# First attention of a two-layer block: four buffers of results, single maxima between the scores, parts of the maxima kept in PSUM

## The reference, cut to what matters

```python
A1 = jnp.einsum('bhqd,bhkd->bhqk', Q1, K1) * scaling
A2 = jnp.einsum('bhqd,bhkd->bhqk', Q2, K2) * scaling
A1 = jnp.where(causal, A1, neg_inf)
A2 = jnp.where(causal, A2, neg_inf)
attn = jax.nn.softmax(A1, -1) - lam * jax.nn.softmax(A2, -1)
O = jnp.einsum('bhqk,bhkd->bhqd', attn, V)
```

## Time and profile before

| | before |
|---|---|
| median of three executions | 4490.27 us |
| lowest and highest | 4481.56 and 4502.51 us |
| the profiled execution | 4483.99 us (span 4481.8 us) |
| mean granted clock of TensorE | 0.902 |
| TensorE busy, whole span | 3649.0 us (81%) |
| VectorE, ScalarE, GpSimd busy | 2374.4, 1656.8, 1702.6 us |
| the attention stage | 354 to 2777 us |

### The profile page before, as it was taken

How to read it: one execution, slowest core, us unless ns; L and a number is a source line. 1 busy time by engine, 2 the same in 40 slices (tenths; PEclk the granted TensorE clock), 3 DMA queues, 4 the chain that set the end, 5 groups by cost and what they waited for, 6 DMA issues and landing times. The chain is left out here.

```text
span 4481.8 us, 84217 instructions
## 1 busy us (share of the span) xinstructions
PE 3649.0 (81%) x28333; PEld 1946.0 (43%) x28335; DVE 2374.4 (53%) x4499; ACT 1656.8 (37%) x3266; POOL 1702.6 (38%) x1117
## 2 busy tenths in 40 slices
PE   6868888998988888888898897762799768897694
PEld 3323344443434343434344443662455434555463
DVE  4457566565656565656566560776511176666202
ACT  2314555555555555555555555110022132111110
POOL 1313454554545454545454555420144332110112
PEclk8978999999999999999999998775699989997797
DMA  4430101111111111111111111210233310001333
GB/s 151 154 113 24 41 25 42 26 40 28 38 30 35 32 34 34 31 37 25 42 26 40 27 26 51 103 48 11 90 90 76 59 34 4 0 0 38 108 100 92
DMA packets 229259, 224.74 MB, mean 50 GB/s; under 512 B 88721, under 2 KB 198546, under 8 KB 222738
## 3 DMA queue, kind: packets, MB, share of 16 engines
q1 hardware_dynamic: 213522, 194.33, 14.7%
q0 software_dynamic: 15360, 25.44, 2.9%
HBM read 138.58 MB, written 80.35 MB: 49 GB/s over the span
## 5 line engine op out<-in xcount | busy, mean ns | idle before, releaser
L692 DVE TENSOR_REDUCE attention_chunk_max<-attention_ps_m 128x1 f32<-128x512 f32 (+3 forms) x2560 | 1386.9, 603 | 892.1 <-PE attention_ps_m L795 451.0
L637 POOL TENSOR_TENSOR attention_probs<-attention_probs 128x1024 f32<-128x1024 f32 (+2 forms) x640 | 1225.9, 1916 | 1281.5 <-PE attention_ps_o L770 1281.5
L670 ACT ACTIVATE attention_probs<-attention_ps_s 128x512 f32<-128x512 f32 (+3 forms) x2560 | 1241.6, 536 | 939.3 <-PE attention_ps_s L745 481.9
L741 PE MATMUL attention_ps_s<-attention_q_stack,attention_k_stack 99*128 99x512 bf16 (+3 forms) x2560 | 836.6, 358 | 176.3 <-ACT attention_probs L670 155.5
L792 PE MATMUL attention_ps_m<-attention_k_stack,attention_q_stack 96*128 96x512 bf16 (+3 forms) x2560 | 811.3, 360 | 152.6 <-DVE attention_chunk_max L692 98.4
L770 PE MATMUL attention_ps_o<-attention_probs,attention_v_head 128*32 128x256 f32 (+1 forms) x9728 | 657.4, 376 | 0.5 <-ACT attention_probs L670 0.4
L792 PEld LDWEIGHTS attention_ps_m<-attention_k_stack,attention_q_stack 96*128 96x128 bf16 x2560 | 248.5, 99 | 524.5 <-DVE attention_chunk_max L692 357.7
L741 PEld LDWEIGHTS attention_ps_s<-attention_q_stack,attention_k_stack 99*128 99x128 bf16 x2560 | 223.2, 98 | 524.1 <-ACT attention_probs L670 259.3
L781 PE MATMUL attention_ps_o<-attention_probs,consts 128*32 128x256 f32 (+1 forms) x5120 | 432.6, 369 | 0.4 <-POOL attention_probs L637 0.4
L770 PEld LDWEIGHTS attention_ps_o<-attention_probs,attention_v_head 128*32 128x32 f32 x9728 | 268.1, 112 | 273.7 <-ACT attention_probs L670 100.4
L781 PEld LDWEIGHTS attention_ps_o<-attention_probs,consts 128*32 128x32 f32 x5120 | 204.4, 113 | 90.3 <-issue 13.5
(11 more groups left out here) (276 smaller groups left out, 3979.6 us busy)
## 6 DMA issues: line engine op xcount, KB each, us to landing
qk_parts<-project_parts SPq DMA_DIRECT2D x64, 384.0 KB, 3.0
heads_out<-attention_results_sb SPq DMA_DIRECT2D x256, 64.0 KB
out_heads<-heads_out SPq DMA_DIRECT2D x8, 2048.0 KB, 7.9
experts_w<-in_f_w SPq DMA_DIRECT2D x16, 1024.0 KB, 8.3
attention_q_stack<-qk_parts SPq DMA_DIRECT2D x32, 384.0 KB
attention_k_stack<-qk_parts SPq DMA_DIRECT2D x32, 384.0 KB
experts_w<-in_e_w SPq DMA_DIRECT2D x24, 512.0 KB, 4.9
v_rows<-project_v SPq DMA_DIRECT2D x8, 1024.0 KB
```

What stands on the lines that cost most here:

```text
L637: pool.tensor_tensor(probs[:, to, :, lo:], probs[:, to, :, lo:], probs[:, k % RING_P, :, lo:], ALU.add).then_inc(pair_ok, 1)
L670: act.activation(probs[:, k % RING_P, a, left(k):], ps_s[(2 * k + a) % RING_S][:, left(k):], ACT.Exp, scale=float(DH) ** -0.5).then_inc(pr ...
L692: last = dve.tensor_reduce(chunk_max[:, a, jq, c:c + 1], ps_m[m % RING_M][:, 0:width(m)], AX.X, ALU.max)
L741: last = pe.matmul(psum[:, lo:], ks[at][0:WITH_MAX, a, kb * P:(kb + 1) * P], qs[at][0:WITH_MAX, a, tq * GROUP + lo:(tq + 1) * GROUP], star ...
```

## The change

- Results: four buffers in SBUF (`RING_R`) and four semaphores `stored` instead of two; a `take` waits for the store of the same turn of the head before. PSUM keeps two (`RING_O`).
- `take` moves from ahead of exponential (k, 1), four steps behind a turn's end, to ahead of exponential (k, 0), five steps behind it.
- The maxima of a pair are cut in four shares (of four: one each; of five: 1, 1, 1, 2). Order in an iteration: score (k + 2, 0), score (k + 2, 1), first share, score (k + 3, 0), second share, `values`, `ones`, third share, score (k + 3, 1), fourth share. In the last pair, the next head's scores (0, 0) and (0, 1) come ahead of the first share and (1, 0) behind the third.
- The split of the maxima works in place in PSUM: no `max_rest`, four chained operations, and the PSUM buffer is released behind the fourth (it was behind the second).

```diff
--- before.py
+++ after.py
@@ -501,16 +501,15 @@
 
 
     with stage(nc, "attention0") as s:
-        RING_P, RING_S, RING_M, RING_O = 8, 3, 3, 2
+        RING_P, RING_S, RING_M, RING_O, RING_R = 8, 3, 3, 2, 4
         qs = [s.sb(f"q_stack{i}", [P, 2, N], BF16) for i in range(STACKS)]
         ks = [s.sb(f"k_stack{i}", [P, 2, N], BF16) for i in range(STACKS)]
         vh = [s.sb(f"v_head{i}", [P, K_TILES, DV], F32) for i in range(STACKS)]
         probs = s.sb("probs", [P, RING_P, 2, GROUP], F32)
-        results = s.sb("results_sb", [P, RING_O, 2, BLOCKS, P], F32)
+        results = s.sb("results_sb", [P, RING_R, 2, BLOCKS, P], F32)
         chunk_max = s.sb("chunk_max", [P, 2, K_TILES, Q_TILES], F32)
         neg_max = s.sb("neg_max", [P, 2 * K_TILES], F32)
         max_parts = s.sb("max_parts", [2 * K_TILES, 3, P], BF16)
-        max_rest = s.sb("max_rest", [2 * K_TILES, P], F32)
         ps_s = [s.ps(f"ps_s{i}", [P, GROUP]) for i in range(RING_S)]
         ps_m = [s.ps(f"ps_m{i}", [P, GROUP]) for i in range(RING_M)]
         ps_o = [s.ps(f"ps_o{i}", [P, 2, BLOCKS, P]) for i in range(RING_O)]
@@ -519,7 +518,7 @@
         (ready, score_ok, prob_ok, values_ok, pair_ok, ones_ok, max_ok, max_used, steps, neg_ok, parts_ok,
          parts_in, taken) = (s.sem(n) for n in names)
         loaded = [s.sem(f"loaded{i}") for i in range(STACKS)]
-        stored = [s.sem(f"stored{i}") for i in range(RING_O)]
+        stored = [s.sem(f"stored{i}") for i in range(RING_R)]
         block = s.engines()
         N_STEPS, N_MAX = len(STEPS), len(MAXIMA) + 1
         LOADS = len(RUNS[0]) + len(RUNS[1]) + 1
@@ -606,7 +605,7 @@
 
             def store(head, turn):
 
-                tile, slot = TURNS[turn - 1], (turn - 1) % RING_O
+                tile, slot = TURNS[turn - 1], (turn - 1) % RING_R
                 h = head - 1 if turn == 0 else head
                 h = h if isinstance(h, int) else sp.snap(h)
                 wait_apart(sp, taken, head * Q_TILES + turn + RING_O, core.passed)
@@ -619,12 +618,12 @@
                         results[half * 2 * DV:(half + 1) * 2 * DV:DV, slot, 1]).then_inc(stored[slot], 16)
 
 
-            for slot in range(RING_O):
+            for slot in range(RING_R):
                 sp.sem_inc(stored[slot], STORES * 16)
             sp.sem_inc(parts_in, 48)
             run(sp, step)
-            for slot in range(RING_O):
-                sp.wait_ge(stored[slot], STORES * 16 * (1 + HEADS * Q_TILES // RING_O))
+            for slot in range(RING_R):
+                sp.wait_ge(stored[slot], STORES * 16 * (1 + HEADS * Q_TILES // RING_R))
 
         @block.gpsimd
         def _(pool):
@@ -645,14 +644,11 @@
             act.sem_inc(taken, RING_O)
 
             def take(head, turn):
-                slot = turn % RING_O
-                if isinstance(head, int):
-                    act.wait_ge(stored[slot], ((head * Q_TILES + turn) // RING_O + 1) * (STORES * 16))
-                else:
-                    act.wait_ge(stored[slot], (head * (Q_TILES // RING_O) + turn // RING_O + 1) * (STORES * 16))
+                slot = turn % RING_R
+                act.wait_ge(stored[slot], (head * (Q_TILES // RING_R) + 1) * (STORES * 16))
                 act.wait_ge(values_ok, head * N_STEPS + LAST[turn] + 1)
                 act.wait_ge(ones_ok, head * PAIRS + (LAST[turn] + 1) // PAIR + RING_P // PAIR)
-                act.activation(results[:, slot], ps_o[slot][:], ACT.Copy).then_inc(taken, 1)
+                act.activation(results[:, slot], ps_o[turn % RING_O][:], ACT.Copy).then_inc(taken, 1)
 
             def step(at_head, after, later):
                 if at_head is None:
@@ -660,8 +656,8 @@
                 head = at_head.n
                 for k in range(N_STEPS):
                     for a in range(2):
-                        ended = ends(k, 4)
-                        if a == 1 and ended and not (ended[1] and is_first(head)):
+                        ended = ends(k, 5)
+                        if a == 0 and ended and not (ended[1] and is_first(head)):
                             take(head - 1 if ended[1] else head, ended[0])
                         act.wait_ge(score_ok, head * 2 * N_STEPS + 2 * k + a + 1)
                         if k % PAIR == 0 and a == 0:
@@ -697,17 +693,17 @@
                         dve.tensor_reduce(neg_max[:], chunk_max[:].rearrange("p a j c -> p (a j) c"), AX.X, ALU.max,
                                           negate=True).then_inc(neg_ok, 1)
 
-                        chain = Counted(dve, steps, after * 2)
+                        chain = Counted(dve, steps, after * 4)
                         m = len(MAXIMA)
                         psum = ps_m[m % RING_M][0:2 * K_TILES, 0:P]
                         dve.wait_ge(max_ok, after * N_MAX + m + 1)
                         dve.wait_ge(parts_in, (after + 1) * 48)
                         chain.then(dve.tensor_copy(max_parts[:, 0], psum))
-                        dve.tensor_tensor(max_rest[:], psum, max_parts[:, 0], ALU.subtract).then_inc(max_used, 1)
-                        dve.wait_ge(max_used, after * N_MAX + m + 1 + RING_M)
-                        chain.then(dve.tensor_copy(max_parts[:, 1], max_rest[:]))
-                        dve.tensor_tensor(max_parts[:, 2], max_rest[:], max_parts[:, 1], ALU.subtract)\
-                            .then_inc(parts_ok, 1)
+                        chain.then(dve.tensor_tensor(psum, psum, max_parts[:, 0], ALU.subtract))
+                        chain.then(dve.tensor_copy(max_parts[:, 1], psum))
+                        chain.then(dve.tensor_tensor(max_parts[:, 2], psum, max_parts[:, 1], ALU.subtract))
+                        dve.sem_inc(parts_ok, 1)
+                        dve.sem_inc(max_used, 1)
 
             def step(at_head, next_head, later):
                 if at_head is None:
@@ -824,30 +820,31 @@
                     if whose is not None and (k == BEGIN_MAX or k == 0 and is_first(head)):
                         pe.wait_ge(loaded[whose_at], (whose.round + 1) * (LOADS * 16))
                     more = k + 2 < N_STEPS
-                    third = -(-len(items) // 3)
+                    share = [items[n * len(items) // 4:(n + 1) * len(items) // 4] for n in range(4)]
                     if more:
                         score(head, at, k + 2, 0)
-                        maxima(whose_n, whose_at, items[:third])
                         score(head, at, k + 2, 1)
-                        maxima(whose_n, whose_at, items[third:2 * third])
+                    maxima(whose_n, whose_at, share[0])
+                    if more:
                         score(head, at, k + 3, 0)
                     elif after is not None:
 
                         pe.wait_ge(parts_in, (after + 2) * 48)
-                        maxima(whose_n, whose_at, items[:2 * third])
                         score(after, other, 0, 0)
+                        score(after, other, 0, 1)
+                    maxima(whose_n, whose_at, share[1])
                     values(head, at, k)
                     values(head, at, k + 1)
                     if k > 0:
                         ones(head, k // PAIR - 1)
                     elif not is_first(head):
                         ones(head - 1, PAIRS - 1)
+                    maxima(whose_n, whose_at, share[2])
                     if more:
                         score(head, at, k + 3, 1)
                     elif after is not None:
-                        score(after, other, 0, 1)
                         score(after, other, 1, 0)
-                    maxima(whose_n, whose_at, items[2 * third:])
+                    maxima(whose_n, whose_at, share[3])
                     if after is not None and k == END_MAX:
                         turn_maxima(after)
                 if after is None:
```

## The result

The changed kernel takes 4107.76 us, the median of four executions (4102.68 to 4111.56), against 4491.16 for the kernel before on the same chips (four executions now). The ratio is 0.9145 with a 95% interval of 0.9121 to 0.9169. That is 383 us less, where 405 were forecast, and inside the likeliest case's own range. The profiled execution has a span of 4104.3 us.

The account below looks back on a forecast made before the run. TensorE's own order of work and its waits bound the attention stage. Gains of 206 + 190 + 7 = 403 us gave 4081 from the profiled 4483.99 and 4087 from the median 4490.27; forecast 4085 us, range 4035 to 4195.

Parts of the forecast that it names:

- likeliest case: Whole kernel: all gains arrive, 4085 us, own range 4040 to 4150, chance 0.72.
- The store stall: ScalarE's copy of results: four buffers end its wait for the store, gaining 206 us, bounds 177 and 231.
- The order: TensorE's pairs of steps: single maxima between scores gain 190 us, bounds 0 and 227; heads 0 and 30 add about 7.
- the 0.5 us for exponentials: TensorE's undisturbed head: 0.5 us added for waits on exponentials, within the forecast 62.0 us.
- The turn of the loop: Turn of the three-head loop: 0.8 us of the mean head's loss, read apart from the clock's 1.0.
- The copy one exponential later: ScalarE's four copies a head: moving them costs nothing; without the move the third score waits some 0.5 us at each.
- The parts in PSUM: VectorE's split of the maxima: casts from PSUM at 0.28 us instead of 920 ns, 0 on the path.
- (a): Rival: the stall goes but waits for exponentials replace those for maxima, so the order brings nothing; 4284 us, chance 0.06.
- (c, d): Rivals at step 20: TensorE waits for a later head's loads; c 4175 us, chance 0.06; d slower, 4560 us, chance 0.02.
- (b): Rival: half of the gain from TensorE's new order is lost; 4184 us, chance 0.10.
- (e): Rival: a copy still waits for a store because SyncE is blocked longer; order gives its 190; 4293 us, chance 0.03.
- under 50 us: Profile sign: TensorE's wait for the maxima in the attention stage falls under 50 us.

Follow-up runs that it names:

- the run with the early wait: The changed kernel with one more TensorE wait, for the loads of the head after the next already at step 12 instead of 20: 4372.33 us.
- the run with the scores in a row: The changed kernel with no maxima between the scores, two shares ahead of the values and two behind the sums: 4304.72 us.

## Why the prediction was right, point by point

**The store stall.** Forecast 206 us, measured 202 alone. Putting an undisturbed head together from a disturbed one and the one head without loads gave 68.54 us, and the chip gave 68.53.

**The order.** Forecast 190 + 7 us on top of the buffers, measured 4289.1 - 4107.8 = 181. The undisturbed head came out at 62.36 us where 62.0 was forecast, 0.36 x 29 = 10 us. It wasn't the 0.5 us for exponentials: the matmuls' waits for them are 4.8 us in the stage, 0.17 a head. Part of it is in the price of the columns. The sum has 14.7 us each for scores and maxima, 68 times 512 columns; at its own price of 0.22 that is 15.0, and the head would have been 62.5. No row separates the rest. Also, four pairs of 19 have five maxima, not a quarter of them, and nothing hangs on that. What the gain is made of was seen in part: of 6.2 us a head 1.8 are the wait behind the split of the maxima (the prediction had about 1.5 for it), and the other 4.4 the bursts in the pairs. The heads outside the loop gave a little more than forecast: head 0 went from 87.64 to 80.25 us, and heads 30 and 31 together gave 2.3, where 7 was forecast for head 0 and head 30.

**The turn of the loop: the term that was mis-sized.** I took the turn's 0.8 us a head over unchanged. It is 63.78 - 62.36 = 1.42 after, and 0.6 x 29 = 18 us went there. In rows: TensorE's eight gaps are 26.1 us where they were 16.1, and behind a gap of 3.4 us it runs at 1.2 GHz (0.53) for as long. Before the change the granted clock stayed at 1.00 through four of the eight turns; after it, it fell at all eight. In the profiled executions the gain is 12.71 x 29 + 7.4 (head 0) + 2.3 (heads 30 and 31) = 378 us where 403 were forecast: 10 and 18 us less by these two items, 3 more by the heads outside the loop. The loop is the cause of the gaps (two turns, two gaps; no loop, no gap), and the loads' DMAs are not. The order makes them longer: they are 25.7 us with the order alone and 18.0 with the buffers alone. Why it does stays open; what I have not tried is what TensorE has queued at the branch.

**The copy one exponential later.** Nothing on the path, as forecast. But I wrote that without the move the third score would wait 0.5 us at each copy, and the run without it shows no cost that can be told from none (4111.39 against 4107.16 us). The step that failed: I priced the copy against the old order, where the score follows the sums at once, and not against the new, where a maximum stands between them.

**The parts in PSUM.** 0, as forecast. On VectorE alone the move pays: 278 against 920 ns for the same cast, and the 920 were the end of GpSimd's sum, as the rows of the two engines in the section on the result show. In the new order that is 0.65 us a head that nobody waits for.

**The rivals.** The exponentials (a) had their price right, 0.42 us a pair, and their condition too: it falls due only without maxima between the scores. The loads (c, d) decided nothing, by 4 to 5 us in a typical head and by about 1 us in the tightest, and the run with the early wait shows that they are through 27.2 us behind their issue, where I had read 27.1 from the store blocked behind them. A stall that moves did show, but in the order alone: 47 us are missing there, 28.5 of them in ScalarE's longer wait. Of (b) and (e) nothing came: the order brought 181 of its 197 us, and no copy waits for a store.

**What the profile was to show.** The clock is 0.99 in the stage, not 1.00, because of the loop's turns (without the loop it is 1.00 from 361.5 to 2307.3 us). Pairs of four full maxima take 3.34 us. The forecast of "under 50 us" for TensorE's waits for maxima is right for matmuls (3.6 us) and wrong for weight loads (181.0 us). It should have named the row. Waits for exponentials are 4.8 us on matmuls and 103.7 on weight loads, not 15 to 40.

## What to carry to other kernels

Before pricing a new order of work, write out one period of the old one from the starts of its instructions and see that it adds up to the measured period; the latency through a ring (here 1.17 us through three buffers of maxima, 1.07 through three of scores) then tells how much other work has to stand between its uses. Take a stall's removal and a better order as one change: the order alone lets the engine run into the stall sooner. Of loops in hardware, look at the gap at the turn again whenever the order of the body changes.

## What the runs showed of the hardware that was not expected

The turn of a hardware loop costs TensorE a gap of about 2.0 us before the change and 3.3 after (26.1 / 8), and with the lower clock behind it (63.78 - 62.36) x 29 / 8 = 5.1 us a turn. Writing out all 32 heads (eight were written before, three of them in the loop) costs the heads nothing measurable: every one of the heads 1 to 28 takes 62.35 or 62.36 us. (Outside the heads the profiled execution of that kernel is 5 us longer than the changed kernel's. One pair of executions can't say more of this, as those of the changed kernel lie 9 us apart.) A small cast on VectorE from SBUF, 0.21 us by itself, lasts until GpSimd's running sum has ended; the same cast from PSUM beside such a sum takes 0.28. Wait rows of weight loads can be large and mean little (181.0 us where the matmuls' own wait is 3.6), or mean a real loss (397.8 us in the run with the scores in a row): the distances between the matmuls' starts decide.
